# Two chunks of level sums and four shift chains placed among attention's steps, in a graph-attention kernel on one core

## The reference

```python
hW = h @ W                                  # per head
hp = (node_adj > 0) @ hW;  hm = (node_adj < 0) @ hW
e_plus = leaky_relu(concat([hp, hm]) @ a)   # one score per node
att = where(edge_adj > 0, e_plus[None, :], NEG_INF)
att = softmax(att, axis=1)
out_head = (att * edge_adj) @ hW            # heads averaged, then a GRU cell
```

## Time and profile before

| what | value |
|---|---|
| median of 3 runs | 1446.94 us (1446.6 to 1449.61) |
| profiled execution, its own time | 1447.55 us |
| its span in the trace | 1444.5 us |
| PE busy | 1351.0 us (94%) |
| DVE busy | 1062.0 us (74%) |
| ACT busy | 909.6 us (63%) |
| POOL busy | 46.2 us (3%) |
| 16 DMA engines, mean | 158 GB/s |

### The profile page before, as it was taken

The page is one execution under the profiler, slowest core; times in us unless marked ns, Lnnn a source line. Parts: engine busy times, 40 slices in busy tenths (PEclk is TensorE's granted clock), DMA queues, the critical chain, the costliest instruction groups (busy, mean ns, idle before and its releaser), DMA issues. The chain is left out here.

```text
span 1444.5 us, 11276 instructions
## 1 busy us (share of the span) xinstructions
PE 1351.0 (94%) x3652; PEld 616.4 (43%) x3652; DVE 1062.0 (74%) x1312; ACT 909.6 (63%) x952; POOL 46.2 (3%) x68
## 2 busy tenths in 40 slices
PE   5999999798799999999999999999979967999996
PEld 4444444255344444444444444444434433444442
DVE  1344333446799999999999999999828868475773
ACT  2655455313598788888878888888625546465553
POOL 0000000100010010010100100100000000000000
PEclk9999999989899999999999999999989978999998
DMA  7878888213224233332333424231062108878822
GB/s 261 333 275 275 286 275 288 60 35 158 103 87 151 98 116 131 102 146 88 125 123 105 143 88 160 88 108 66 1 243 83 44 4 320 317 294 299 300 98 60
DMA packets 53823, 228.80 MB, mean 158 GB/s; under 512 B 9928, under 2 KB 15752, under 8 KB 36232
## 3 DMA queue, kind: packets, MB, share of 16 engines
q1 hardware_dynamic: 51200, 225.55, 44.0%
q10 hardware_dynamic: 2568, 2.58, 0.5%
HBM read 223.82 MB, written 4.29 MB: 158 GB/s over the span
## 5 line engine op out<-in xcount | busy, mean ns | idle before, releaser
L1115 PE MATMUL t_y_ps<-mask,x_sb 128*128 128x512 f32 x1536 | 666.2, 596 | 15.2 <-DVE mask L1045 15.2
L1115 PEld LDWEIGHTS t_y_ps<-mask,x_sb 128*128 128x128 f32 x1536 | 293.1, 191 | 385.0 <-issue 368.1
L1045 DVE TENSOR_TENSOR mask<-mask 128x1536 f32<-128x1536 f32 x256 | 450.0, 1759 | 2.1 <-ACT mask L893 2.1
L893 ACT ACTIVATE mask<-mask,ones 128x1536 f32<-128x1536 f32 x256 | 399.3, 1560 | 1.1 <-DVE mask L1031 1.1
L886 ACT ACTIVATE mask<-mask,t_minus_e 128x512 f32<-128x512 f32 x256 | 184.6, 721 | 89.9 <-PE t_y_ps L1115 88.2
L1031 DVE TENSOR_SCALAR mask<-mask,e_cols 128x512 f32<-128x512 f32 x512 | 228.5, 488 | 13.7 <-PE t_y_ps L1115 9.9
L282 PE MATMUL ns_ps<-pieces,x_sb 128*128 128x512 f32 x512 | 229.0, 603 | 7.0 <-POOL pieces L150 7.0
L1682 PE MATMUL p_ff_ps<-mask,p_g_all 128*128 128x512 f32 x512 | 223.8, 598 | 9.1 <-ACT mask L1621 9.1
L1682 PEld LDWEIGHTS p_ff_ps<-mask,p_g_all 128*128 128x128 f32 x512 | 97.6, 192 | 129.5 <-issue 120.3
L282 PEld LDWEIGHTS ns_ps<-pieces,x_sb 128*128 128x128 f32 x512 | 96.7, 193 | 129.6 <-issue 129.4
L167 ACT ACTIVATE signs<-pieces 128x2048 fp8e4<-128x2048 f32 x64 | 122.3, 1911 | 46.7 <-DMA pieces<-in_adj_c 25.3
(11 more groups left out here) (178 smaller groups left out, 629.8 us busy)
## 6 DMA issues: line engine op xcount, KB each, us to landing
pieces<-in_adj_c SPq DMA_DIRECT2D x64, 1024.0 KB, 5.0
mask<-in_adj_c SPq DMA_DIRECT2D x64, 1024.0 KB, 4.8
mask<-in_adj_t SPq DMA_DIRECT2D x32, 2048.0 KB, 8.7
mask<-scratch_shifts SPq DMA_DIRECT2D x8, 1536.0 KB, 8.1
pieces<-in_x_t SPq DMA_DIRECT2D x1, 2048.0 KB, 11.5
scratch_ns_t<-ns_sb ACTq DMA_DIRECT2D x8, 256.0 KB, 5.9
p_g_x_t<-in_x_t SPq DMA_DIRECT2D x8, 256.0 KB, 2.9
p_g_ns_t<-scratch_ns_t SPq DMA_DIRECT2D x8, 256.0 KB, 3.1
```

The lines of the kernel that those rows point to most:

```text
L893: nc.scalar.activation(t, t, ACT.Exp, bias=ones[:, :], scale=-1.0).then_inc(exped, 1)
L1045: nc.vector.tensor_tensor(term(n), term(n), a, ALU.mult).then_inc(terms, 1)
L1115: mm = nc.tensor.matmul(y_ps[c % 2][h][:, :], x_sb[:, k, :], term(n)[:, h, :], start=k == 0, stop=k == NB - 1)
```

## The change

`EARLY = 6` chunks of level sums stay ahead of the steps. Those of chunk 6 are done by PE after step 5, those of chunk 7 after step 10. DVE does chains 0 to 3, then the first three gaps; chains 4, 5, 6 and 7 stand after steps 1, 4, 10 and 15. The copies, exponentials and transposes that belong to them are spread over steps 2 to 25.

```diff
+EARLY = 6
 # ACT
-            for c in range(NCHUNK - 1):
+            for c in range(EARLY - 1):
                 take_out(c)
                 if c:
                     shift_exps_of(c - 1)
                 if c >= 2:
                     rows_out(c - 2)
             act.wait_ge(negated, 1)
-            last = NCHUNK - 1
-            among = {0: lambda: shift_exps_of(last - 1), 1: lambda: (take_out(last), rows_out(last - 2)), 3: lambda: rows_out(last - 1),
-                     4: lambda: shift_exps_of(last), 10: lambda: rows_out(last)}
+            among = {2: lambda: (take_out(5), shift_exps_of(4)), 3: lambda: rows_out(3), 6: lambda: shift_exps_of(5), 7: lambda: rows_out(4),
+                     10: lambda: take_out(6), 12: lambda: shift_exps_of(6), 13: lambda: rows_out(5), 15: lambda: take_out(7),
+                     17: lambda: shift_exps_of(7), 20: lambda: rows_out(6), 25: lambda: rows_out(7)}
 # DVE
-            for c in range(NCHUNK - 2):
+            for c in range(EARLY - 2):
                 chain(c)
             for n in range(AHEAD):
                 gap(n)
-            chain(NCHUNK - 2)
+            chains = {1: 4, 4: 5, 10: 6, 15: 7}
             for n in range(NB * NCHUNK):
                 ...
                 make_terms(n)
-                if n == 1:
-                    chain(NCHUNK - 1)
+                if n in chains:
+                    chain(chains[n])
 # PE
-            for c in range(NCHUNK):
+            def level_sums(c):
                 ...
-                    if k == 7 and c:
+                    if k == 7 and 0 < c < EARLY:
                         turn_sums(c - 1)
-                    if k == 24 and c >= 2:
+                    if k == 24 and 2 <= c < EARLY:
                         turn_shifts(c - 2)
                 mm.then_inc(sums_done, 1)
+            for c in range(EARLY):
+                level_sums(c)
             last = NCHUNK - 1
-            among = {0: lambda: turn_sums(last), 1: lambda: turn_shifts(last - 1), 8: lambda: turn_shifts(last)}
+            among = {2: lambda: turn_sums(5), 3: lambda: turn_shifts(4), 5: lambda: level_sums(6), 7: lambda: (turn_sums(6), turn_shifts(5)),
+                     10: lambda: level_sums(7), 12: lambda: turn_sums(7), 15: lambda: turn_shifts(6), 20: lambda: turn_shifts(7)}
```

## The result

The changed kernel takes 1443.93 us (median of 10 runs, 1441.53 to 1447.29), beside it the kernel before 1448.82 us. The ratio is 0.9966 with a 95% interval of 0.9952 to 0.998: 4.9 us less, between 2.9 and 7.0. Forecast was 3.6 us less. In a second group of runs the ratio was 0.9962 (0.9948 to 0.9976), 5.5 us less. (The ratio is an estimate over all runs of a group, so it need not be the quotient of the medians; in the second group these are 4.05 us apart.)

The account below looks back on a forecast made before the run. PE was taken to bound the steps, DVE 4% behind. Waste from 20.3 to 14.65 us gains 5.6, less 2.0 for one clock fall: 3.6 us off the median 1446.94, 1443.3 us; range for 8 in 10 1440.5 to 1446.2.

Parts of the forecast that it names:

- The waste: PE's idle and slow time at the steps' start: 20.3 us before, 14.65 after, plus 2.0 for the clock.
- What bounds: PE bounds the attention steps at 2.575 us each, DVE needs 2.46; later stages move along with the middle phase's end.
- Steps 0 to 2: PE idles 1.35 us ahead of step 0 and 5.2 ahead of step 2, which then loses 2.55 at half clock.
- Chain 5 and step 5: PE idles 3.1 us ahead of step 5; 4.7 if step 2 ran at full clock, changing the sum by 1 only.
- The lead at step 16: From step 16 on, DVE's lead over PE is zero in both kernels, counted back by 2.46 us a step.
- The sums' cover: Level sums of chunks 6 and 7 hide chain 6 at no cost; without them it costs about 3 us.
- Chain 7 and step 16: Chain 7 after step 15 makes PE idle 2.45 us ahead of step 16.
- The clock: Behind the short idles ahead of steps 5 and 16, one fall to half clock, 2.0 us; bounds for both 0 and 5.1.
- rival B: Clock falls behind both short idles, ahead of steps 5 and 16: gain 1.6 us, 1445.3 us; chance 0.24.
- Rival C: ACT late for chains 4, 5 and 7, 3.1 us each: 1450.6 us; decides beyond 2.2 us late; chance 0.08.
- Queues and loads: Later shift and piece loads on SP stay hidden by 40 us; ACT's small work doesn't wait; step 36 stays as is.
- The walk: The prediction's step-by-step timeline of PE, DVE and ACT from chain 3 to step 16, giving each idle.

Follow-up runs that it names:

- the fillers: Changed kernel plus 41, 40 and 19 useless PE matmuls behind steps 1, 4 and 15; 1440.84 us, ratio 0.9946 against the kernel before.
- The run with the sums at step 7: Changed kernel with chunk 7's level sums behind step 7 instead of step 10; 1448.14 us, ratio 0.999 against the kernel before.
- the chains ahead: Changed kernel with chains 4 and 5 put back ahead of the steps, level sums left behind steps 5 and 10; 1446.68 us, ratio 0.9972 against the kernel before.
- the sums behind step 1: Changed kernel with chunk 6's level sums behind step 1 instead of step 5; 1434.67 us, ratio 0.9899 against the kernel before.
- One pair late: Changed kernel with ACT's exponentials for chains 4, 5 and 7 one step later, behind steps 3, 7 and 18; single execution, 1443.55 us.
- two pairs: Changed kernel with ACT's exponentials for chain 4 alone two steps later, behind step 4; 1446.94 us, ratio 0.9983 against the kernel before.
- another order: Changed kernel with chains 4 to 7 behind steps 4, 8, 12, 16 and sums of chunks 6, 7 behind steps 3, 9; 1434.53 us, ratio 0.9893 against before.

## Why the prediction was right

**How near.** The forecast time, 1443.3 us, is closer to the measured 1443.93 than the forecast gain, 3.6 us, is to the measured 4.9: it was taken from a median of three runs, 1446.94, and the ten runs beside the changed kernel had 1448.82. The waste was forecast at 14.65 + 2.0 = 16.65 us and measured 16.5, and that closeness is partly luck: the idles were 12.1 us forecast and 11.2 measured, the half clock 4.55 forecast and 5.3 measured.

**What bounds.** Right: PE's idle and slow time at the steps' start is the whole change. From the first combine to the end the spans are 964.9 us before and 963.5 after, mostly by the clock at the last combine (4.54 and 2.84 us, see the end), where nothing was changed.

**Steps 0 to 2.** Idles ahead of them 1.35 and 5.2 us in the forecast, 1.28 and 4.88 measured.

**Chain 5 and step 5.** 3.1 forecast, 2.81 measured. Its rule, that a faster step 2 would only lengthen this idle to 4.7, was shown by the fillers (4.44).

**The lead at step 16.** The prediction counted back from step 36 by 2.46 us a step and found no lead. That left out `scale_y` (1.88 us at 461.87): multiply 16 of the kernel before ends at 414.33, 0.9 us ahead of PE's step 16. The sum doesn't use it.

**The sums' cover.** Right, the size somewhat high: without it chain 6 was priced at about 3 us. The run with the sums at step 7 lost 2.7, 2.0 of it in the two idles behind the edit.

**Chain 7 and step 16.** 2.45 forecast, 2.26 measured.

**The clock.** Here the sizes were off, in both directions. Step 2's restart was priced at 2.55 us like those of before and cost 1.80. For the two short idles I counted one fall of 2.0; in the profile both fell, 1.80 and 1.70. That is rival B in its mechanism, but 3.4 us in size, where B said 1.6, because each fall was cheaper and the idles were 0.9 us shorter. So the term for the clock (one fall) was wrong for both profiles of this kernel, and a cheaper fall at step 2 (0.75 us) and shorter idles (0.9 us) made up for it. In other orders the clock held after the same idles (2.27 us with the chains ahead, 2.81 us with the sums behind step 1). Whether it also does in some executions of the changed kernel isn't shown: no profile caught it, and the interval of 2.9 to 7.0 us can't choose.

**Rival C.** Its mechanism is real and its decision point was placed well: margins 2.1, 2.2 and 2.6 us forecast, 2.10, 1.49 and 2.57 measured. One pair late cost 0.3 us for three chains, two pairs cost 1.9 us for one. Its price of 3.1 us a chain was read from a chain that was held for another reason as well (ACT waited 4.32 us for the transposed shifts) and was too high for this.

**Queues and loads.** No wait for a shift or a piece appeared on DVE or ACT among the steps; right.

**What the prediction missed** is no step of the sum: that DVE waits 9.1 us for free slots while PE waits 11.2 us for DVE. The walk had the hold in it (gap 12 waits for step 6) and called the cover free. PE has no idle there, so the sum holds; but the same sums beside chain 4 would have covered an idle of 4.88 us, as the run with them behind step 1 shows.

## What to carry to other kernels

When two engines both are near their bound, follow both through the same stretch: if each waits for the other at different moments, try the order before the amount of work; here the same instructions in another order took 10.8 us more off the stretch. It paid to put PE's filling work where DVE runs a chain, and to keep the chains apart by four steps. A filler for PE can be worth its place even where it computes nothing, but only as a test: real work in the first of the three places was worth about twice as much (6.7 us without the clock's luck, against 3.4 for fillers in all three).

## What the runs showed of the hardware

**The same idle, two outcomes.** Behind an idle of 2.05 us the last combine of attention took 4.54 us in the kernel before and 2.84 us in the changed one:

```profile
1053.87 2.84 PE L1086 MATMUL t_es_ps<-mask,t_gat_w 128*128 128x512 f32 x6 [2.05 <-DVE mask L1020]
```

Six instructions of the same shape, the same idle, no edit near them: 1.7 us. Over all eleven profiles this combine was slow in four (4.31 to 4.54 us) and at full clock in seven. Idles of 2.26 to 2.27 us ahead of step 16 were followed by half clock in four profiles and by full clock in one, 2.81 us ahead of step 5 by half in five and by full in one; 1.83 us and less never cost anything among the steps, 4.0 us and more did each time that no filler stood there. A fall among the steps cost 1.4 to 2.6 us, and 3.0 in the run with the chains ahead, where PE had done little but three small groups of transposes for 14 us. The Trainium skill, "TensorE: Matmul & The Clock Gate", section "Part 1: The HAM clock gate", says that the number of slow matmuls varies between runs of one kernel; the traces agree: the first 40 level sums, the same code behind the same 9.0 us idle, took 10.23 to 11.78 us. Behind the short idles here even whether any are slow varies.

**Where part of the spread can come from.** The 4.7 us by which the level sums start later in the profile after lie at the kernel's very start. Windows before and after of 28 to 34 and 34 to 40 us:

```profile
28.00:34.00 6.00, 6.00 (x18) 4.13 (x18) 1.94 (x6) 0.00 (x0) 0.00 (x0) 0.55 0.42 132
34.00:40.00 6.00, 6.00 (x15) 2.66 (x14) 2.46 (x2) 4.01 (x4) 0.00 (x0) 1.00 1.01 426
```

```profile
28.00:34.00 6.00, 6.00 (x29) 6.00 (x30) 0.07 (x1) 0.00 (x0) 0.00 (x0) 0.50 0.01 3
34.00:40.00 6.00, 6.00 (x8) 2.44 (x9) 3.11 (x7) 1.35 (x1) 0.00 (x0) 0.55 0.84 321
```

The same code, PE busy throughout, and in the second execution it is at half clock for some 5 us longer. In the profiles of all kernels the level sums started between 291.2 and 293.2 us or between 295.4 and 296.1 us; the changed kernel's two profiles are both late, but a reordered one starts at 291.9, and the kernel before is early alone and late with fillers. That is as large as the change, and it is why the profile's whole span can't show it and the stretch can. That it also makes the spread of the times without a profile isn't shown, though that spread is of the same size (1446.6 to 1452.15 us for the kernel before).
